# Second attention: 24 stack transfers a batch become 12 with twice the packet, heads h and h + 8 side by side, and the projections move to other steps

## The reference, cut to what matters

```
xn = layernorm(x)
# attention: 16 heads, q and k of 16 features, v of 8
q, k, v = xn @ Wq.T, xn @ Wk.T, xn @ Wv.T        # per head
qf, kf = taylor_exp(q), taylor_exp(k)             # qf . kf = 1 + s/4 + s*s/32, with s = q . k
A = tril(qf @ kf.T)                               # causal
s = ((A @ v) / (sum over A's row + 1e-12)) @ Wo.T
# coupling network, three cycles over the whole x
for _ in range(3):
    tf = sigmoid(gelu(gelu(gelu(out@w1+b1)@w2+b2)@w3+b3)@w4+b4)
    out = out + (0.1 + r*(0.7*gf + 0.3*tf - 0.5)*2) * twist(out)   # twist swaps the channel halves
x = x + s * silu(out)
```

## Time and profile before

| what | before |
|---|---|
| median of 3 runs | 997.2 us (994.97 to 1000.61) |
| profiled execution, its own time | 995.62 us |
| its span | 993.8 us |
| PE busy | 908.0 us (91%) |
| DVE busy | 692.7 us (70%) |
| ACT busy | 635.3 us (64%) |
| POOL busy | 367.9 us (37%) |
| stack transfers in the second attention | 192 of 128.0 KB |
| coupling network | 628 to about 718 us |
| second attention | 715 to 994 us |

### The profile page before, as it was taken

One profiled execution on the slowest core, in us unless ns is written; L12 is line 12 of the kernel. 1 busy time (PEld: TensorE's weight loads), 2 busy tenths in 40 slices (PEclk: granted clock), 3 DMA queues, 4 the chain that ended last, 5 costly groups with the idle time before them and its releaser, 6 DMA issues. The chain is left out here.

```text
span 993.8 us, 18406 instructions
## 1 busy us (share of the span) xinstructions
PE 908.0 (91%) x6682; PEld 464.0 (47%) x6682; DVE 692.7 (70%) x1052; ACT 635.3 (64%) x1378; POOL 367.9 (37%) x355
## 2 busy tenths in 40 slices
PE   4699999999999999989999988899669999999996
PEld 2233344343444444448888876322224344434443
DVE  7769889998989999603333358786767667767544
ACT  4458677778787878743333223576477878777774
POOL 4012021224353332004666631464556455645200
PEclk9559799999999999989999999999699999999999
DMA  7632425150404000017777462159998999999600
GB/s 229 247 139 98 179 102 209 50 180 27 177 24 175 28 27 22 2 32 231 217 220 213 147 194 64 42 103 141 141 108 83 104 113 102 104 104 112 76 11 22
DMA packets 80958, 114.31 MB, mean 115 GB/s; under 512 B 12930, under 2 KB 57988, under 8 KB 78436
## 3 DMA queue, kind: packets, MB, share of 16 engines
q1 hardware_dynamic: 73668, 94.87, 48.6%
q0 software_dynamic: 6352, 17.86, 5.2%
q10 hardware_dynamic: 848, 0.40, 0.1%
HBM read 56.00 MB, written 33.57 MB: 90 GB/s over the span
## 5 line engine op out<-in xcount | busy, mean ns | idle before, releaser
L962 DVE TENSOR_REDUCE a_nmax<-quad 128x2 f32<-128x1024 f32 x256 | 301.9, 1219 | 36.2 <-PE quad L573 34.0
L772 ACT ACTIVATE a_probs<-bank 128x512 f32<-128x512 f32 x339 | 190.9, 598 | 55.2 <-PE bank L590 32.5
L1830 ACT ACTIVATE a_late<-quad 128x256 f32<-128x256 f32 (+3 forms) x512 | 180.4, 463 | 40.3 <-PE quad L1618 39.5
L1970 DVE SCALAR_TENSOR_TENSOR a_late<-a_late,const 128x512 f32<-128x512 f32 x128 | 116.7, 919 | 76.0 <-ACT a_late L1830 75.6
L602 PE MATMUL av<-a_probs,a_va 128*32 128x256 f32 x2048 | 168.1, 401 | 0.9 <-ACT a_probs L772 0.6
L573 PE MATMUL quad<-k_stack,q_stack 24*128 24x512 f32 x512 | 133.6, 525 | 9.4 <-DVE a_nmax L962 5.0
L590 PE MATMUL bank<-q_stack,k_stack 26*128 26x512 f32 x339 | 136.9, 507 | 4.2 <-DMA q_stack<-a_nparts 2.8
L772 ACT ACTIVATE a_probs<-misc 128x512 f32<-128x512 f32 x173 | 103.3, 597 | 23.9 <-PE bank L590 12.4
L1247 POOL DMA_INDIRECT expert_rows<-m_ob,m_xr x78 | 75.4, 966 | 106.3 <-DVE m_ob L1357 78.5
L1618 PE MATMUL quad<-q_stack,k_stack 96*128 96x256 bf16 (+3 forms) x512 | 104.2, 304 | 7.7 <-ACT a_late L1830 3.7
L1629 PE MATMUL av<-a_late,a_va 128*32 128x512 f32 (+3 forms) x1024 | 97.5, 454 | 5.1 <-DVE a_late L1981 4.3
(11 more groups left out here) (280 smaller groups left out, 1383.3 us busy)
## 6 DMA issues: line engine op xcount, KB each, us to landing
m_wu<-packed_weights SPq DMA_DIRECT2D x39, 384.0 KB, 3.7
spread<-a_parts SPq DMA_DIRECT2D x48, 256.0 KB
q_stack<-a_parts SPq DMA_DIRECT2D x96, 128.0 KB, 7.5
k_stack<-a_parts SPq DMA_DIRECT2D x96, 128.0 KB, 7.8
q_stack<-spread SPq DMA_DIRECT2D x7, 1024.0 KB, 5.0
k_stack<-spread SPq DMA_DIRECT2D x7, 1024.0 KB, 7.4
sorted_rows<-in_shape_constants POOLq DMA_DIRECT2D x5, 1040.0 KB, 5.3
m_xr<-sorted_rows SPq DMA_DIRECT2D x39, 130.0 KB, 2.9
```

Source lines behind the costliest of these rows:

```text
L772: act.activation(probs[:, (GH * s + j) % 8, :], col_bank(n)[:, :], ACT.Exp, scale=scale).then_inc(col_free, 1)
L962: dve.tensor_reduce(nmax[quad % 2][:, at:at + 2 * TT:TT], row_slot(n)[:, :, :], AX_X, ALU.max, negate=True)\
L1830: act.activation(probs[:, (64 * b + n) % 12, kt * P:T], quad[:, n % 4, kt * P:T], ACT.Square, bias=1.0, scale=0.25)\
L1970: dve.scalar_tensor_tensor(out=blocks, in0=blocks, scalar=1.0, in1=S["tri"][:, None, :].broadcast_to([P, GH, P]), op0=ALU.add, op1=ALU.mul ...
```

## The change

The pieces are now counted k = 0, 1 for queries (heads 0 to 7, heads 8 to 15) and k = 2, 3 for keys. The `parts` buffers have the two halves of the heads side by side, and the stacks keep heads h and h + 8 next to each other, so that one transfer moves one part of all 16 heads to a row group: 256 KB, packets of 2,048 bytes, six transfers for queries and six for keys. The row groups, 16 partitions each, are the same. `score` reads head h at place 2 * (h % 8) + h // 8.

- Waits: `stack(b, ...)` waits for all scores of batch b - 2 (before: half a for half of them). `cast` waits for the query transfers of the batch before (k = 0, 1), or for its key transfers (k = 2, 3). Batch b's first score waits for both.
- Steps: the pieces are made at t = 6, 7, 11 and 12.
- The border: queries of batch 0 go out two rows at a time behind swaps 6, 7 and 8, its keys behind swaps 12, 13 and 14, the queries of batch 1 behind swaps 18, 19 and 20, and the keys of batch 1 after the last swap. Pieces 4 to 7 are made one group of steps earlier or at the same place.
- In the attention SP stores batch i - 1 first, and then issues both stacks of batch i + 2.

```diff
-        parts = [sb(f"parts{i}", [P, 3, T], BF16) for i in range(4)]
+        parts = [sb(f"parts{i}", [P, 3, 2, T], BF16) for i in range(2)]
...
-        STACK = 16 * 2 * len(PAIRS)
-        EARLY = ((0, 1), (2,), (3,), (), (4,), (5,), (6, 7))
+        STACK = 16 * len(PAIRS)
+        QK_AT = (6, 7, 11, 12)
+        EARLY = ((0, 1), (2,), (3,), (4,), (5,), (6,), (7,))
...
-            def stack(b, par, half, rows=range(len(PAIRS))):
-                done = stack_b if half else stack_a
+            def stack(b, par, op, rows=range(len(PAIRS))):
+                to, of, done = (qs, ks)[op][par], parts[op], stacked[op]
                 wait(sp, done, STACK * b)
-                wait(sp, split, 4 * b + 2 + 2 * half)
-                wait(sp, s_mm, 64 * (b - 2) + 32 * (half + 1))
-                heads = slice(8 * half, 8 * half + 8)
+                wait(sp, split, 4 * b + 2 * op + 2)
+                wait(sp, s_mm, 64 * (b - 1))
                 for n in rows:
-                    for op, (dst, part) in enumerate(((qs, PAIRS[n][0]), (ks, PAIRS[n][1]))):
-
-                        sp.dma_start(dst[par][DQ1 * n:DQ1 * (n + 1), heads, :], parts[2 * half + op][:, part, :]).then_inc(done, 16)
+                    sp.dma_start(to[DQ1 * n:DQ1 * (n + 1), :, :].rearrange("r (h two) t -> r h (two t)", two=2),
+                                 of[:, PAIRS[n][op], :, :].rearrange("p two t -> p (two t)")).then_inc(done, 16)
...
             for n in range(ALL):
                 swap(n)
-                if B <= n < B + 2 * len(PAIRS):
-                    half, row = divmod(n - B, len(PAIRS))
-                    stack(0, 0, half, (row,))
-            stack(1, 1, 0)
+                if 6 <= n < 9:
+                    stack(0, 0, 0, (2 * (n - 6), 2 * (n - 6) + 1))
+                if 12 <= n < 15:
+                    stack(0, 0, 1, (2 * (n - 12), 2 * (n - 12) + 1))
+                if 18 <= n < 21:
+                    stack(1, 1, 0, (2 * (n - 18), 2 * (n - 18) + 1))
             stack(1, 1, 1)
             for i in range(B):
-                if i + 2 < B:
-                    stack(i + 2, i % 2, 0)
                 if i >= 1:
                     store(i - 1)
                 if i + 2 < B:
+                    stack(i + 2, i % 2, 0)
                     stack(i + 2, i % 2, 1)
...
+                h = 2 * (h % 8) + h // 8
                 if t == 0 and j == 0:
-                    wait(pe, stack_a, STACK * (b + 1))
-                if t == 8 and j == 0:
-                    wait(pe, stack_b, STACK * (b + 1))
+                    wait(pe, stacked[0], STACK * (b + 1))
+                    wait(pe, stacked[1], STACK * (b + 1))
...
-                    if n <= 5 and t in (1, 2, 11, 12):
-                        q_k(i + 2, par, t - 1 if t < 8 else t - 9)
+                    if n <= 5 and t in QK_AT:
+                        q_k(i + 2, par, QK_AT.index(t))
...
-                wait(dve, stack_b if half else stack_a, STACK * b)
-                dve.tensor_copy(parts[k][:, 0, :], full[op][:, :]).then_inc(qk_cast, 1)
+                wait(dve, stacked[k // 2], STACK * b)
+                dve.tensor_copy(parts[k // 2][:, 0, k % 2, :], full[k % 2][:, :]).then_inc(qk_cast, 1)
```

More of the change, by code:

```diff
@@ L1544, in split_one @@
             def split_one(c, k):
-                f, r, pt = full[k % 2], rest, parts[k]
+                f, r, pt = full[k % 2], rest, parts[k // 2][:, :, k % 2, :]
                 wait(pool, qk_cast, c + 1)
@@ L1593, in q_k @@
             def q_k(b, par, k):
-                half, op = k // 2, k % 2
+                op, half = k // 2, k % 2
                 w = S["wk1T"] if op else S["wq1T"]
@@ L1813, in read_qk @@
             def read_qk(b, k):
-                half, op = k // 2, k % 2
                 wait(act, qk_mm, 4 * b + k + 1)
                 wait(act, split, 4 * b + k - 1)
-                act.activation(full[op][:, :], (S["misc"] if b < 2 else misc2)[:, :], ACT.Copy).then_inc(qk_read, 1)
+                act.activation(full[k % 2][:, :], (S["misc"] if b < 2 else misc2)[:, :], ACT.Copy).then_inc(qk_read, 1)
             def squares(b, t):
@@ L1857, in main @@
                         read_o(i, par, 0)
-                    if n <= 5 and t in (1, 2, 11, 12):
-                        read_qk(i + 2, t - 1 if t < 8 else t - 9)
+                    if n <= 5 and t in QK_AT:
+                        read_qk(i + 2, QK_AT.index(t))
                     if t == 7 and n >= 1:
@@ L2015, in main @@
                         read_gate(t - 3)
-                    if n <= 5 and t in (1, 2, 11, 12):
-                        cast(i + 2, t - 1 if t < 8 else t - 9)
+                    if n <= 5 and t in QK_AT:
+                        cast(i + 2, QK_AT.index(t))
                     if t in (4, 5) and n >= 1:
```

3 lines of the change are left out of this document (1 added, 2 removed).

## The result

The changed kernel takes 1011.1 us (median of 4 runs, 1005.6 to 1014.8); the kernel before, run beside it, 997.8 us (4 runs, 995.0 to 1000.6). The ratio is 1.0156, 95% interval 1.012 to 1.0192: slower, as forecast, and inside the stated range of 984 to 1015, but by 13 us between the medians and 16 between the two profiled spans (1010.0 and 993.8) where 8 to 9 were forecast. The forecast of 1005 is too low by 6 us, and the prediction's own narrower range, 999 to 1011, just misses the median.

A forecast was written before the change was run, and what follows sets the result against it. It took the DMA queue to bound the coupling network, and the chain of scores, squares, masks and weighing the attention. +4 us to batch 1's start and +5 in the batches on 995.6 gave 1004.6, forecast 1005; range 984 to 1015.

The forecast's parts named there:

- The rate of the stacks: Stack transfers: 110 GB/s with the larger packets too, since each still goes to 16 partitions.
- The coupling network: Longer transfer queue from swap 6 makes the last product end later: +7 us, 4 to 9.
- The border: Behind the last product: a 1.49 us cast moves earlier and a 2.67 us cast wait goes; step 3's scores at about 731.
- Batch 0: First attention batch: two query pieces moved to steps 6 and 7 cost 0.5 us; batch 1 starts +4 later.
- The batches: Attention batches 1 to 5: late key casts and moved projections together cost +1.0 us a batch, +5 in all.
- I take 0.9: Step 11 of an attention batch: the key cast waits for late keys, losing 0.2 to 1.3 us, taken as 0.9.
- I take +0.1, near what they cost now: Attention batches: moving two projections from steps 1 and 2 to 6 and 7 costs +0.1 us, bounds -0.6 to +1.6.
- Batch 6 should keep its 31.5: Attention batch 6, without casts: its length stays 31.5 us.
- A: Rival: larger packets double the stacks' rate to 220 GB/s, no cast waits for keys; 984 us, chance 0.18.
- B: Rival: rate 110 GB/s, but swap slack and masks absorb the delays, or projections are cheaper; 998 us, chance 0.2.
- C: Rival: batches locked to the queue, key cast delay passed on in full, +2.8 us a batch; 1015 us, chance 0.1.
- The signs that were named: Trace signs: rate near 110 GB/s, last product 722 to 727, batch 1 at 757 to 764, periods 33.2 to 34.5 us.

The follow-up runs named there:

- a1: Changed kernel with each stack transfer cut into two of 1,024-byte packets to the same 16 partitions; ratio 1.0215 to the kernel before.
- a2: Changed kernel with stack row n laid to every sixth partition instead of 16 neighbours; ratio 1.0007 to the kernel before.
- a3: Changed kernel with the query transfers of batch 1 issued after the last swap; ratio 1.0088 to the kernel before.
- b2: Kernel before with only the projections of steps 1 and 2 moved to steps 6 and 7; ratio 1.0078 to the kernel before.
- a4: Changed kernel with the key projections at steps 13 and 14 instead of 11 and 12; ratio 1.0135 to the kernel before.
- b1: Kernel before with only stack row n laid to every sixth partition, 1,024-byte packets kept; ratio 0.9867 to the kernel before.
- a5: Changed kernel with stack rows on every sixth partition and transfers cut into two of 1,024-byte packets; ratio 1.0 to the kernel before.
- b1 again: The same kernel as b1, run a second time as a yardstick; ratio 0.989 to the kernel before.
- c2: b1 with its projections of steps 11 and 12 moved to 13 and 14; ratio 0.988 to the kernel before.
- a7: Changed kernel with seven extra matmuls ahead of the first weighted values of batch 0; ratio 1.0162 to the kernel before.

## Why the prediction was right in direction and half in size

- **The rate of the stacks: right.** 110 forecast; 112 to 116 measured over the sets, 116 in the window. "The narrow target is the likelier brake" was an inference; a1 and a2 show it: packets +4 to 6%, placement x 1.8 to 1.9. The Trainium skill, page "SBUF — State Buffer", section "Door 1: The DMA port swizzle", gives about 109 GB/s for 16 neighbouring partitions, and nothing in it depends on the packet; the runs agree, with 102 to 113 for small and 112 to 116 for large ones. For the spread rows its table puts at most two of a row's 16 partitions on one port, as with 8 ports evenly used, an estimate of 218 GB/s; a2's sets measured 200 to 216, and a window of ten microseconds 225.
- **The coupling network: right, a little small.** +7 (4 to 9) forecast, +8.8 measured. a3 splits it: 6.6 for the six rows of batch 1, 2.2 for the rest.
- **The border: the number right, half of the reason wrong.** From the last product to the scores of step 3 it is 9.2 to 6.4 us, -2.8; the forecast's own times, 725 to 731, made it -3.2. 1.3 of that is the cast of 1.49 us, as forecast. But the cast's wait of 2.67 us, which was said to hold the mask and then the scores, held no scores: they wait for squares and for PE, and PE ran without a gap from `weigh(0)` over the projection of step 2 to them. The other 1.5 us are that projection, gone to step 6; b2 has the same 1.5, and has its cast of 1.48 us where it stood. That the number fits is luck.
- **Batch 0: the step that failed first.** "The two query pieces, at steps 6 and 7, cost another 0.5": behind step 3 it was +4.9. By b2 the move is worth 1.9 there, two projections at 0.96 in steps that have no wait for them; of the two places they left, step 1 lay in PE's long wait for the border and was free (`weigh(0)` starts 5.85 us behind the last product in the kernel before and in b2 alike), and step 2 gave back the 1.5 us at the border. The rest goes with the half clock, 1.5 in steps 3 to 5 and 1.6 at step 10, which makes the 4.9 but for rounding; the sum had no term for it. From the last product to batch 1 the forecast had -3, and it was +2.2.
- **The batches: sum nearly right, terms exchanged.** +1.0 a batch forecast, +1.36 measured. But "I take 0.9" for the late key cast was 0.45 (0, 1.0 and three times 0.4), and "I take +0.1, near what they cost now" for the moved projections was 0.91. b2, a2 and a4 agree on this. The bound that was given, +1.6, held it. The two terms are not independent: the move makes steps 11 to 15 later. The cast of step 11 starts 26.30 us into a batch before, and 27.34 in a2, where it waits for no transfer; keys at 28.7 are then 1.4 us late and not the 2.4 of the old schedule, against which the 0.9 was worked out. No run has late keys with the projections at steps 1 and 2, so that 0.9 would have held there is not shown. The two errors nearly cancel in the sum, which is luck too.
- **Slips in the working.** The stated starts and rates put the keys at 28.7 us (-1.1 + 1.2 + 28.6), where the casts in fact started at 28.1 to 29.3, and not at 29 to 29.1. With the shorter durations the mask of step 13 ends at 31.3 (30.2 + 0.43 + 0.69), before its `weigh` asks for it, so nothing lost was a possible outcome, where the text has 0.2 as the least. And slices 27 to 36 of the earlier trace rows move 83 to 141 GB/s; the 76 is slice 37.
- **What led the +0.1 astray is a row.** It was worked out from the batch without pieces, 31.50 us in the earlier trace rows, whose granted clock is 0.95. Such a batch lasts 29.97 at the full clock (the changed kernel, and b1, which has none of the change), so four projections cost 2.7, not 1.2, and the prediction's own bound, two at 1.12 less what two cost now, becomes +0.9 instead of +1.6. Measured was 0.91. "Batch 6 should keep its 31.5" fell with it: a1, a changed kernel, lasts 31.6 there, with a half clock inside that its window shows, and b1 30.0. The -1.6 is no gain of the change.

```profile
945.00:976.00 31.00, 29.57 (x233) 12.79 (x233) 17.57 (x28) 23.26 (x67) 6.92 (x7) 0.94 1.02 102
```

- **The rivals.** A's premise was wrong, and a2 shows its price was too: with twice the rate the changed kernel only equals the kernel before. B is wrong: the longer queue came through, the masks took up the late cast in one batch of five, and the projections are dearer at steps 6 and 7. C is wrong in the batches, where 0.45 of 2.8 was passed on. The measured 1011.1 lies nearer to C's 1015 than to 1005 all the same; its mechanism is not what did it.
- **The signs that were named.** The rate, the periods (33.58 to 34.55 for 33.2 to 34.5) and, by 0.15 us, the last product (727.15 for 722 to 727) came out. Batch 1 started at 767.9, not by 764; the key casts waited 0.7 to 1.4 us, not 2 to 3; two query casts waited where none should; the transfers of a set ended some 6 us before the end of the batch, not in its last 4.

Together: 8.8 - 2.8 + 4.9 + 6.8 - 1.6 = 16.1 for the span's 16.2. What of the half clock in batch 0 belongs to the change and what to the single execution stays open: step 10 ran at the full clock in the kernel before, a4, a5 and b2 and at half in all the others, with and without the change, which no single edit sorts. The stretch ahead of it reached 1.6 to 4.2 us into step 3 where the projections are moved, and -0.4, -0.2, +2.0 and +2.0 where they are not (before, b1, b1 again, c2). a7 removed neither.

## To carry to other kernels

Before a piece of work is moved on the bound engine, ask what the engine does in the slots it leaves and in those it enters, wait by wait: a projection cost 0.05 us beside a 0.8 us wait and 0.9 to 0.96 without one, and in the first batch, whose wait was several us long, one projection lay inside the wait and was free, while the next lay just behind it and cost 1.5 us at half the clock. When two terms of a sum move the same step, price the second in the schedule that the first one leaves: here the keys came 1.4 us late for it, and 2.4 by the old one. When a price is derived as the difference of two stretches, compare them at the same granted clock, or the clock ends up in the price. And where a queue is full at half the rate of its neighbours, look at which partitions a transfer writes before its packets: one slice in one line was worth 1.1 to 1.3%, where this whole change cost 1.6.

## What the runs showed of the hardware

- With packets of 2,048 bytes a copy within SBUF into 16 neighbouring partitions moves 112 to 116 GB/s (changed kernel), into 16 partitions six apart 200 to 216 over whole sets (a2) and 225 in a window, at 150 and 75 us of engine time for a MB.
- With spread targets 1,024-byte packets cost the engines no more for a MB (60 us, a5) than 2,048-byte ones (75, a2); transfers of 128 KB are then held by SP, which issues one every 0.65 us (a5).
- Extra matmuls in a wait of PE did not keep the full clock behind it (a7): the half-clock stretches came at other places, and the time was the same.
- A half-clock stretch of 3.4 us cost 1.6 us where PE is bound (batch 6 of the kernel before and of a1; step 10 of batch 0 of the changed kernel) and 0.95 in steps 6 to 9 of batch 0 (b1 again). The end of a longer one, which reached 2.0 us into steps 3 to 5, cost 1.2 (b1 again against b1).
